# Keys of two batches in one product in the cross-attention of a float32 transformer block

## The reference

```python
q = (x @ Wq).reshape(b, n, HEADS, D_HEAD)          # 16 heads of 64
k = (ctx @ Wk).reshape(b, m, HEADS, D_HEAD)        # m = 120, ctx has 192 columns
v = (ctx @ Wv).reshape(b, m, HEADS, D_HEAD)
sim = jnp.einsum('bihd,bjhd->bhij', q, k) * SCALE
attn = jax.nn.softmax(sim, axis=-1)
out = jnp.einsum('bhij,bjhd->bihd', attn, v).reshape(b, n, HEADS * D_HEAD)
return out @ Wo + bo
```

## Time and profile before

| what | value |
|---|---|
| median of 3 runs | 954.59 us (954.51 to 954.76) |
| profiled execution | 959.5 us, span 957.7 us |
| TensorE busy | 904.8 us, 94% |
| VectorE busy | 758.3 us, 79% |
| ScalarE busy | 671.0 us, 70% |
| GpSimd busy | 392.3 us, 41% |
| TensorE's granted clock, mean | 0.987 |
| self-attention, batches 0 to 7 | about 141 to 524 us of the span |
| cross-attention, batches 8 to 15 | about 524 to 803 us |
| feed-forward | from about 803 us |

### The profile page before, as it was taken

One profiled execution on the slowest core, in us unless ns is written; L12 is line 12 of the kernel. 1 busy time (PEld: TensorE's weight loads), 2 busy tenths in 40 slices (PEclk: granted clock), 3 DMA queues, 4 the chain that ended last, 5 costly groups with the idle time before them and its releaser, 6 DMA issues.

```text
span 957.7 us, 21112 instructions
## 1 busy us (share of the span) xinstructions
PE 904.8 (94%) x7200; PEld 841.2 (88%) x7200; DVE 758.3 (79%) x1650; ACT 671.0 (70%) x2009; POOL 392.3 (41%) x506
## 2 busy tenths in 40 slices
PE   7999998999999999999998998899999987999998
PEld 6788787898989999999987888899899977999998
DVE  5887779888888888888897887888988886466664
ACT  5677658778777777777787778778878886233433
POOL 1215535343434443434443655656556655010010
PEclk9999998999999999999999999999999998899999
DMA  7231002142111111111132135122212213110100
GB/s 233 77 114 40 16 24 62 35 87 71 34 35 35 35 35 40 35 35 40 29 80 77 42 76 112 45 49 60 56 38 59 57 41 82 34 33 25 34 24 23
DMA packets 85746, 51.67 MB, mean 54 GB/s; under 512 B 43273, under 2 KB 79113, under 8 KB 85641
## 3 DMA queue, kind: packets, MB, share of 16 engines
q1 hardware_dynamic: 85640, 50.32, 21.1%
HBM read 41.64 MB, written 8.65 MB: 53 GB/s over the span
## 4 chain that ended last, share of the span: by engine, by line
PE 71%; ACT 9%; DVE 8%; issue 4%; DMA 4%; POOL 1%; SPq 1%; DVEq 0%; POOLq 0%; ACTq 0%
PE bank L1476 10%; PE bank L1477 9%; PE bank L1478 9%; PE bank L1741 6%; PE bank L1721 5%; PE bank L1493 4%; PE bank L1770 4%; PE bank L1771 4%; ACT p L834 3%; PE bank L1789 3%; PE bank L1791 3%; PE bank L1790 3%; DMA rsums_dram<-rsum 3%; PE bank L1597 2%; PE bank L1598 2%
## 5 line engine op out<-in xcount | busy, mean ns | idle before, releaser
L622 POOL TENSOR_TENSOR oT_scaled<-oT,rsumT 128x256 f32<-128x256 f32 x128 | 97.1, 759 | 293.5 <-DVE oT L1276 165.8
L834 ACT ACTIVATE p<-bank,negmax 128x256 f32<-128x256 f32 (+1 forms) x512 | 207.6, 427 | 13.9 <-DVE negmax L1239 10.3
L1476 PE MATMUL bank<-hT_hi,w_hi 128*128 128x256 f32 x640 | 189.9, 297 | 6.9 <-DVE qkT_lo L1308 2.7
L1477 PE MATMUL bank<-hT_lo,w_hi 128*128 128x256 f32 x640 | 180.3, 282 | 0.0
L1478 PE MATMUL bank<-hT_hi,w_lo 128*128 128x256 f32 x640 | 180.2, 282 | 0.0
L1476 PEld LDWEIGHTS bank<-hT_hi,w_hi 128*128 128x128 f32 x640 | 122.8, 192 | 11.4 <-issue 9.2
L1477 PEld LDWEIGHTS bank<-hT_lo,w_hi 128*128 128x128 f32 x640 | 122.3, 191 | 0.0
L1478 PEld LDWEIGHTS bank<-hT_hi,w_lo 128*128 128x128 f32 x640 | 122.2, 191 | 0.0
L844 ACT CAST pT_hi<-bank 128x512 fp32r<-128x512 f32 x128 | 68.9, 591 | 68.4 <-PE bank L1741 68.3
L1770 PE MATMUL bank<-pT_hi,v_hi_lo 128*128 128x256 f32 (+1 forms) x384 | 99.7, 288 | 16.3 <-DVE oT L1276 14.4
L834 ACT ACTIVATION_READ_ACCUMULATOR p<-bank,negmax 128x1 f32 x512 | 110.3, 215 | 0.0
(11 more groups left out here) (204 smaller groups left out, 2726.6 us busy)
## 6 DMA issues: line engine op xcount, KB each, us to landing
rsumT<-rsums_dram SPq DMA_DIRECT2D x256, 64.0 KB, 3.0
w_stage<-in_weights SPq DMA_DIRECT2D x47, 256.0 KB, 4.9
x_in<-x_dram SPq DMA_DIRECT2D x24, 256.0 KB, 4.4
x_dram<-x_out SPq DMA_DIRECT2D x16, 256.0 KB, 3.5
l_x<-in_x SPq DMA_DIRECT2D x4, 512.0 KB, 5.0
x_dram<-l_out SPq DMA_DIRECT2D x4, 512.0 KB, 2.8
rsums_dram<-rsum SPq DMA_DIRECT2D x128, 2.0 KB, 3.3
out_dram<-x_out SPq DMA_DIRECT2D x8, 256.0 KB, 2.1
```

The lines of the kernel that those rows point to most:

```text
L622: nc.gpsimd.tensor_tensor(on[:, :].rearrange("p (t q) -> p t q", t=NT), of[:, G % DEEP, :].rearrange("p (t q) -> p t q", t=NT), rT[:, G % ...
L834: last = nc.scalar.activation(p[:, G % 2, e, t * cols:(t + 1) * cols], scores_at(G, e, t), ACT.Exp, bias=negmax[:, G % 2, t, e:e + 1], acc ...
L1476: nc.tensor.matmul(dst, lh, rh, start=(i == 0), stop=False)
L1477: nc.tensor.matmul(dst, lh, rl, start=False, stop=False)
```

## The change

From batch 10 on, the batches go in pairs (10, 11), (12, 13), (14, 15). The keys of both batches of a pair are computed in one product: the weights stay, and the moving operand is both contexts side by side, 240 columns. The eight groups are cut in four key products of two groups (`project_two_keys`, j = 0 to 3) for a pair of batches. Before, each batch had two products of four groups at 120 columns. Batches 8 and 9 keep their own keys.

The odd batch's keys go to a second block-diagonal set, `kdh2` and `kdl2`. It lies in the halves of the value tile and of the transposed-probability tile that the cross-attention doesn't use; all these tiles are now parts of one, `HL`. GpSimd zeroes this second set in steps 4 and 5 of batch 8, in eight further memsets, and the first zeroing of the first set moves from step 4 to step 5 of batch 7. The contexts' tiles are joined, so that two stand side by side.

The steps of TensorE, and with them the roundings on ScalarE and the subtractions on VectorE, become:

| i | batches 8, 9 | even, 10 to 14 | odd, 11 to 15 |
|---|---|---|---|
| 0 | keys (b, 1) | two-batch keys 2 | values (b, 1) |
| 1 | queries (b, 2); in batch 9 values (9, 1) before them | queries (b, 2) | queries (b, 2) |
| 2 | queries (b, 3) | two-batch keys 3 | queries (b, 3) |
| 3 | values (8, 1) in batch 8; context 11 in batch 9 | queries (b, 3) | context b+2 |
| 4 | keys (9, 0) in batch 8; two-batch keys 0 in batch 9 | values (b, 1) | two-batch keys 0 of b+1 |
| 5 | queries (b+1, 0), values (b+1, 0) | the same | the same |
| 6 | queries (9, 1) in batch 8; two-batch keys 1 in batch 9 | queries (b+1, 1) | two-batch keys 1 of b+1 |
| 7 | context 10 in batch 8; queries (10, 1) in batch 9 | context b+2 | queries (b+1, 1) |

Batch 15 has nothing that belongs to a next batch. The output projection and the `prepare` transposes keep their steps. The transfer of the context of batch b+2 is issued in step 0 of an odd batch and in step 5 of an even one. Waits follow the new order. Those of note: queries of an even batch wait for the low parts of the two-batch keys of the same index; queries (b, 2) of an odd batch, 9 included, wait for the low parts of values (b, 1); value products (b, 1) of even batches use bank 7.

```diff
+def cross_order():
+
+    order = [("k", B, 0), ("q", B, 0), ("q", B, 1), ("k", B, 1), ("q", B, 2), ("q", B, 3)]
+    order += [("k", B + 1, 0), ("q", B + 1, 0), ("q", B + 1, 1), ("k", B + 1, 1), ("q", B + 1, 2), ("q", B + 1, 3)]
+    for b in range(B + 2, 2 * B, 2):
+        order += [(w, b, c) for c in range(4) for w in "kq"] + [("q", b + 1, c) for c in range(4)]
+    return {what: PAIRS * B + n + 1 for n, what in enumerate(order)}
+
+
+CROSS = cross_order()
+
+
+def two_batches(b):
+
+    return b >= B + 2
...
-    return PAIRS * B + 6 * (b - B) + (2, 2, 3, 3, 5, 5, 6, 6)[g]
...
+    if two_batches(b):
+        return max(key_product(b - b % 2, g // 2), query_product(b, g // 2))
+    return max(key_product(b, g // 4), query_product(b, g // 2))
...
-            ch = sb("cT_hi", [128, KT, SC], F32R, where=l1)
-            cl = sb("cT_lo", [128, SC], F32R, where=l1)
+            ch = sb("cT_hi", [128, KT, 2, SC], F32R, where=l1)
+            cl = sb("cT_lo", [128, 2, SC], F32R, where=l1)
...
+            HL = sb("qk_v_pT", [128, 8 * PAIRS * S], F32R, where=l1)
...
+            qch, kdh, qcl, kdl, kdl2, kdh2 = (part(n, 1).rearrange("p (g n) -> p g n", g=PAIRS) for n in (0, 1, 2, 3, 5, 7))
+            kh_at, kl_at = (1, 7), (3, 5)
+            pch, pcl = (part(6, 1)[:, n * 4 * S:(n + 1) * 4 * S].rearrange("p (a e n) -> p a e n", a=2, e=2) for n in range(2))
...
+        def kk_bank(j):
+            return bank[7 if j == 0 else 3]
+
+        def kk_src(j, e):
+
+            return kk_bank(j)[e * DH:(e + 1) * DH, 0:4 * SC].rearrange("p (g a n) -> p g a n", g=2, a=2)
+
+        def kk_dst(at, j, e):
+
+            first = at[0] * PAIRS * S + 2 * j * S + e * SC
+            one = HL[e * DH:(e + 1) * DH, first:first + 1]
+            return bass.AP(one.tensor, one.offset, [one.ap[0], [S, 2], [(at[1] - at[0]) * PAIRS * S, 2], [1, SC]])
...
-                if i == 5 and B < b + 2 < 2 * B:
+                if i == (0 if b % 2 and b > B else 5) and B < b + 2 < 2 * B:
...
+                if b == B - 1 and i == 5:
+                    zero_keys(0, G + 1, G - 1)
...
+                if b == B and i in (4, 5):
+                    zero_second_keys(i - 4)
...
+            def two_keys_low(b, j):
+                dve.wait_ge(y["qk_hi"], key_product(b, j))
+                for e in range(2):
+                    last = nc.vector.tensor_tensor(kk_dst(kl_at, j, e), kk_src(j, e), kk_dst(kh_at, j, e).bitcast(F32),
+                                                   ALU.subtract)
+                last.then_inc(y["qk_lo"], 1)
...
+            def project_two_keys(b, j):
+
+                if j == 0:
+                    pe.wait_ge(y["cT_lo"], b + 1 - B + 1)
+                    pe.wait_ge(y["h_full"], KT * (b + 1))
+                else:
+                    pe.wait_ge(y["qk_lo"], query_product(b, j - 1))
+                for g in range(2):
+                    last = context_product(kk_bank(j)[:, g * 2 * SC:(g + 1) * 2 * SC],
+                                           [wcols(A2W + "k", kt, (2 * j + g) * 128, 128) for kt in range(KT)],
+                                           c_both(), True)
+                last.then_inc(y["qk"], 1)
+
...
+                if c == 0 and two_batches(b) and b % 2 == 0:
+                    pe.wait_ge(y["cT_lo"], b + 1 - B + 1)
+                elif c == 0 and two_batches(b):
+                    pe.wait_ge(y["qk_lo"], query_product(b - 1, 3))
+                elif c == 0:
                     pe.wait_ge(y["v_lo"], values_until(b - 1, 7))
+                elif two_batches(b) and b % 2 == 0:
+                    pe.wait_ge(y["qk_lo"], key_product(b, c))
+                elif c == 2 and b > B:
+                    pe.wait_ge(y["v_lo"], value_product(b, 1))
                 else:
...
-                if i == 0:
-                    project_keys(b, 1)
-                if i in (1, 2):
-                    project_queries(b, i + 1)
-                if i == 3:
-                    project_values(b, 1)
-                if i in (5, 6) and more:
-                    project_queries(b + 1, i - 5)
+                if not two_batches(b):
+                    if i == 0:
+                        project_keys(b, 1)
+                    if i == 1 and b == B + 1:
+                        project_values(b, 1)
+                    if i in (1, 2):
+                        project_queries(b, i + 1)
+                    if i == 3 and b == B:
+                        project_values(b, 1)
+                elif b % 2 == 0:
+                    if i in (0, 2):
+                        project_two_keys(b, 2 + i // 2)
+                    if i in (1, 3):
+                        project_queries(b, 2 + i // 2)
+                    if i == 4:
+                        project_values(b, 1)
+                else:
+                    if i == 0:
+                        project_values(b, 1)
+                    if i in (1, 2):
+                        project_queries(b, i + 1)
+                if i == 5 and more:
+                    project_queries(b + 1, 0)
+                if b % 2 == 0 and i == 6:
+                    project_queries(b + 1, 1)
+                if b % 2 == 1 and more and i == 6:
+                    project_two_keys(b + 1, 1)
+                if b % 2 == 1 and more and i == 7:
+                    project_queries(b + 1, 1)
                 if i == 0:
                     project_out(b - 1, 3 if b == B else 5, 6)
                 if i == 1:
@@ -1928,10 +2102,12 @@
                 if i == 2:
                     pe.wait_ge(y["out"], b)
                     prepare(b + 1, 7)
-                if i == 4 and more:
+                if i == 4 and b == B:
                     pe.wait_ge(y["h_full"], KT * (b + 2))
                     project_keys(b + 1, 0)
-                if i == 7 and b + 2 < 2 * B:
+                if i == 4 and more and b % 2 == 1:
+                    project_two_keys(b + 1, 0)
+                if i == (3 if b % 2 else 7) and b + 2 < 2 * B:
                     context(b + 2)
                 if i == 5 and more:
```

183 lines of the change are left out of this document (129 added, 54 removed).

## The result

| | before | after |
|---|---|---|
| median of the runs, us | 954.67 (4 runs, 954.51 to 956.87) | 971.57 (4 runs, 969.31 to 972.64) |
| profiled execution, its span | 959.5, 957.7 | 972.25, 970.5 |
| mean granted clock | 0.987 | 0.981 |
| TensorE, VectorE, ScalarE busy | 904.8, 758.3, 671.0 | 897.1, 759.7, 673.1 |
| batch 9's S to batch 15's S | 204.70 | 220.90 |

The ratio is 1.0175 (95% interval 1.015 to 1.02), 16.9 us, where I had forecast 6.6. The direction was right and the size was not; the time lies above my range. A pair of batches lasts 71.7 us (10 and 11) and 72.1 us (12 and 13), not the 69 that I had forecast.

A forecast was written before the change was run, and what follows sets the result against it. It took VectorE's list, with ScalarE before it, to bound steps 0 to 5 of a batch, and TensorE only steps 5 to 7. Stalls of +5.3 us and clock +1.3 made +6.6: 954.6 becomes 961.2 us, range 951 to 968.

The forecast's parts named there:

- S to X of an even batch: From S (first score matmul, step 0) to X (first query matmul, step 1): stays 6.59 us, change 0.
- V to S of an odd batch: From V (step 5's value product) to the next S (first score matmul): 11.43 us in place of 9.48, +1.95.
- Odd S to X: First score matmul to step 1's first queries in an odd batch: 5.95 us, 0.64 earlier; net -0.45 with GpSimd's wait.
- Step 7's queries of an odd batch: Queries moved to step 7 of batches 9, 11, 13 wait for two-batch keys' low parts, starting at V + 7.79 us.
- Batch 9's queries: Step 1 of batch 9: queries behind the values start at X + 3.6 us, a stall of +3.5.
- Rival 1: TensorE decides after all; the saved 12.6 us, or at least half, come out: 942.0 to 948.3 us; chance 0.17.
- rival 4: The 240-column product isn't cheaper; three pairs pay 4.2 us more on TensorE: 962 to 965, within the forecast's chance.
- Rival 3: The clock falls in all seven places, at up to 1.5 us each: 967 to 970 us; chance 0.10.
- batches 9 and 10 would lose their lateness: Delays of 0.6, 1.6 and 1.4 us there, from small transfers queued behind the weights, vanish with the later schedule.
- Step 3 of an even batch: Weighted values 1.22 us late behind two-batch keys 3; V at X + 18.2 and not 17.53: +0.65 each.
- clock term: TensorE's clock falls to 1.2 GHz in three of seven places with idle gaps, at 0.45 us each: +1.3 us.
- Steps 3 and 4 of an odd batch: TensorE loses values and keys, but VectorE runs with hardly a gap and V waits for its end: -0.2 us each.

The follow-up runs named there:

- e5: Kernel before, with every cross-attention key product cut to 2 of its 5 matmuls per column group: 955.75 us, ratio 0.9984.
- e12: Changed kernel with transposes of the identity filling all of TensorE's long stalls: 968.72 us, ratio 1.0145 to the kernel before.
- e1: Changed kernel with the second half of values of batches 10, 12 and 14 projected, rounded and split earlier in step 4: 967.10 us, ratio 1.0100.
- e3: Changed kernel with the output product ahead of the queries in step 7 of batches 9, 11 and 13: 971.00 us, ratio 1.0145.
- e6: Changed kernel with 16 transposes of the identity in each of four stalls (batch 9 step 1; step 4 of 9, 11, 13): 971.21 us, ratio 1.0137.
- e10: Changed kernel with the scaled hidden state written behind the probabilities' low part and rounded in step 4, in five batches: 972.80 us, ratio 1.0156.
- e14: Changed kernel with three order repairs and odd-step-4 transposes, then half the key rounding and splitting for pairs 4 to 7, batches 12 and 14: 956.86 us, ratio 1.0023.
- changed again: The changed kernel itself, measured a second time as a yardstick: 974.16 us, ratio 1.0176 to the kernel before.

## Why the forecast was too low

**What held.** TensorE's saving was worth nothing by itself: S to X of an even batch 6.59, as forecast, and e5 shows the same where 12.7 us of it are gone. V to S of an odd batch: 11.43 forecast, 11.38 and 11.39 measured. Odd S to X: 5.95 forecast, 5.75 and 6.07 measured. Step 7's queries of an odd batch: V + 7.79 forecast, 7.80 measured in batch 13. Batch 9's queries: X + 3.6 forecast, 3.63 measured, and without the clock (e12) its S to V is 27.56, 2.87 more than before, for which the sum had 2.9. The strided destination was free. Rival 1 is excluded by e5 and by the result, rival 4 by the products themselves: 10 matmuls of 240 columns in 1.20 us where 20 of 120 took 2.26. Rival 3's time, 967 to 970, is nearer to the result than mine, but by luck: the clock is 3.4 us of the 16.9. One reading of mine was not shown by its row: V at 724.91 has no idle time marked before it and stands 0.13 behind the matmul ahead of it, where matmuls in a row stand 0.11 to 0.12 apart, so TensorE and VectorE got there almost together. And that batches 9 and 10 would lose their lateness held in the changed kernel's profile (V to S 11.38 in batch 9, X to V 20.04 in batch 10, both as in the later batches), but is partly luck: one part of it, the wait for `oT_lo`, came in other runs in batch 10, 11 or 14.

**The step that failed: "Step 3 of an even batch", +0.65.** By "TensorE's and VectorE's lists" I brought V to X + 18.2; it came at X + 20.0 to 20.2 in three batches. By their lengths that is 1.83 to 1.98 us more than my sum for each, 5.7 of the 8.4 us by which S9 to S15 exceeds my sum and its clock term. I wrote that step 4 has values in place of keys and counted them as TensorE's 1.23 us. I did not ask who reads them: pair 4, one step later, behind a rounding and a subtraction at the end of both lists. The rows show that low part of the values 1.58 to 1.76 us behind the one that I had taken for the last, and e1 wins 1.2 to 1.35 of it and pays 0.3 for its own place in VectorE's list. The 0.2 us that are left stand already in step 3, where the probabilities' low part ended at X + 12.64 in batch 12 and not at X + 12.44; no run took that apart.

**The clock term, +1.3.** The count was near, four falls in the changed kernel's profiled execution where I had let three of seven fall, but I priced each at 0.45. Against e12 the clock cost 2.2 us in batch 9, for two products: by e1, where only the second fell, 1.5 for the queries behind the stall and 0.7 for the keys of step 4. It cost 0.6 and 0.7 for the keys of step 4 in batches 11 and 13 (35.55 and 35.99 against 34.98 and 35.32 in e12). Together 3.4 against 1.3. Rival 3 (all seven) was wrong in its count, though an even batch's step 5 can fall, as e3, e6 and e10 showed.

**"Steps 3 and 4 of an odd batch", -0.2, and step 0.** Beyond the clock, batches 11 and 13 are 0.2 and 0.4 us longer than the forecast's 34.8 and 34.9. That is small; which of the two terms it is stays open.

**Sum.** Even batches 5.7, clock 2.1 more than taken, odd batches 0.6: 8.4, which is what separates S9 to S15 (16.2 us longer than before) from my 7.8 for it. The medians differ by 16.9.

## What to carry to other kernels

When a product is moved to a later step, walk from it to its first reader through every engine's list, not only through the step that it enters: the moved product cost nothing where I priced it and about 1.6 us a step later, where I had not looked. Computing two batches' keys in one product halves TensorE's time for them and none of their rounding; all four roundings of a pair now come due between step 4 of the odd batch and step 2 of the even one, and where TensorE already waits for such a rounding, the merge adds waits (e14: with two of these roundings halved, the even batches 12 and 14 were 0.7 us shorter than before the change). Such a premise can be tested before the change is written, by leaving the work out of the kernel as it is (e5): 1.6 times the saving was worth at most 3.6 us.

## What the chip showed

The same stall was followed by the lower clock in some executions and not in others. In batch 9 TensorE had 1.28 busy us of 3.40 in the changed kernel, then ran at 0.50 (1.2 GHz), 12 matmuls of 256 columns in 2.70 us; with 1.24 of 3.40 in e1 it stayed at 1.00 (2.4 GHz), and they took 1.47. Of the five profiled executions with this stall unfilled, the clock fell behind it in three (changed, changed again, e10) and not in two (e1, e3). So my reading of two windows of one trace tells where the clock may fall, not that it will. The Trainium skill (TensorE: Matmul & The Clock Gate, Part 1, "The HAM clock gate") says of a kernel's start that the count of matmuls at the lower clock varies from run to run; these rows show the like in the middle of a kernel. At the lower level ten matmuls of 240 columns took 2.27 us in place of 1.20.

Transposes of the identity in the stalls kept the granted clock at 1.00 over 217 us (e12), and no batch from 9 to 14 was longer with them than without: batch 9's S to X was 10.23 with them and 10.22 without, batch 12 lasted 36.04 and 36.07.
